# A disentangled-attention layer in a four-stage kernel: c2p rows in four buffers, c2p tables four units ahead, both skewed reads two units ahead, and fewer of stage 3's loads during attention

## The reference, cut to what matters

```
scores = einsum('bhqd,bhkd->bhqk', q, k) / scale
c2p_att = einsum('bhqd,hpd->bhqp', q, pos_k)              # 128 positions p
c2p = take_along_axis(c2p_att, clip(rel + 64, 0, 127))    # rel: bucket of q - k
p2c_att = einsum('bhkd,hpd->bhkp', k, pos_k)
p2c = swapaxes(take_along_axis(p2c_att, clip(-rel + 64, 0, 127)), -1, -2)
probs = softmax(scores + (c2p + p2c) / scale)
ctx = einsum('bhqk,bhkd->bhqd', probs, v)
```

## Time and profile before

| | us |
|---|---|
| median of 3 runs | 2724.37 |
| lowest, highest | 2719.42, 2726.56 |
| profiled execution, its own time | 2727.48 |
| its span, first to last instruction | 2725.4 |
| mean granted TensorE clock | 0.847 |

### The profile page before, as it was taken

How to read it: one execution, slowest core, us unless ns; L and a number is a source line. 1 busy time by engine, 2 the same in 40 slices (tenths; PEclk the granted TensorE clock), 3 DMA queues, 4 the chain that set the end, 5 groups by cost and what they waited for, 6 DMA issues and landing times. The chain is left out here.

```text
span 2725.4 us, 47318 instructions
## 1 busy us (share of the span) xinstructions
PE 1965.8 (72%) x13556; PEld 1445.9 (53%) x13557; DVE 1632.0 (60%) x4103; ACT 1046.4 (38%) x2098; POOL 898.0 (33%) x1079
## 2 busy tenths in 40 slices
PE   6867777777777777777769999755335159999742
PEld 3435666666666666665646666433225028877421
DVE  8946665666666566665765553577747754444344
ACT  3445554555555555555423223332001163333000
POOL 4122222222222222222232220267630015554656
PEclk9979898998988888888979999777565559999876
DMA  4679998998999899999742110000001414447333
GB/s 149 195 238 287 278 290 262 290 280 271 284 266 281 255 281 269 276 280 282 233 122 62 48 30 1 0 0 0 0 19 47 178 32 155 154 148 139 109 97 110
DMA packets 290039, 456.40 MB, mean 167 GB/s; under 512 B 38608, under 2 KB 225024, under 8 KB 289824
## 3 DMA queue, kind: packets, MB, share of 16 engines
q1 hardware_dynamic: 269344, 398.77, 48.6%
q0 software_dynamic: 16320, 42.39, 6.3%
q10 hardware_dynamic: 4160, 12.58, 1.2%
HBM read 236.67 MB, written 216.92 MB: 166 GB/s over the span
## 5 line engine op out<-in xcount | busy, mean ns | idle before, releaser
L935 DVE CUSTOM_DVE_ANT_0 probs<-bank,c2p 128x512 f32<-128x512 f32 x512 | 351.8, 687 | 425.7 <-PE bank L832 217.9
L893 ACT ACTIVATE probs<-probs,neg_max 128x512 f32<-128x512 f32 x512 | 371.5, 726 | 69.9 <-DVE neg_max L935 69.5
L908 ACT COPY a_stage<-bank 128x320 f32<-128x320 f32 (+1 forms) x512 | 211.9, 414 | 427.1 <-PE bank L801 416.3
L944 DVE COPY probsT<-bank 128x512 f32<-128x512 f32 x512 | 351.2, 686 | 11.0 <-PE bank L842 10.6
L842 PE MATMUL bank<-ident,probs 128*128 128x128 f32 x2048 | 334.7, 289 | 1.0 <-ACT probs L893 0.9
L813 PE MATMUL bank<-tab,k 96*128 96x320 bf16 (+1 forms) x512 | 165.0, 322 | 197.1 <-DVE b_stage L887 149.6
L842 PEld LDWEIGHTS bank<-ident,probs 128*128 128x128 f32 x2048 | 277.3, 152 | 13.1 <-issue 1.8
L771 POOL COPY end_c2p<-a_stage 128x4 f32<-128x4 f32 (+1 forms) x128 | 24.8, 194 | 752.0 <-ACT a_stage L908 596.9
L2122 POOL DMA_INDIRECT p_x_tile<-y_d,p_token x160 | 153.0, 956 | 329.4 <-POOLq L1813 207.4
L832 PE MATMUL bank<-ident,p2c 128*128 128x128 f32 x1280 | 249.1, 296 | 0.0
L827 PE MATMUL bank<-k,q 96*128 96x384 bf16 (+1 forms) x512 | 167.3, 327 | 91.7 <-DMA p2c<-p2c_d 66.2
(11 more groups left out here) (254 smaller groups left out, 3770.0 us busy)
## 6 DMA issues: line engine op xcount, KB each, us to landing
p2c_d<-b_stage SPq DMA_DIRECT2D x64, 640.0 KB, 4.9
c2p_d<-a_stage SPq DMA_DIRECT2D x64, 640.0 KB, 4.5
p2c_d<-b_stage SPq DMA_DIRECT2D x64, 576.0 KB, 5.2
c2p_d<-a_stage SPq DMA_DIRECT2D x64, 576.0 KB, 3.5
p2c<-p2c_d SPq DMA_DIRECT2D x256, 144.0 KB, 4.5
c2p<-c2p_d SPq DMA_DIRECT2D x256, 144.0 KB, 4.3
o_sorted_d<-p_o_pair SPq DMA_DIRECT2D x80, 256.0 KB
k<-k_stack_d SPq DMA_DIRECT2D x192, 64.0 KB
```

The lines of the kernel that those rows point to most:

```text
L893: act.activation(probs[:, w % 2, j, :], probs[:, w % 2, j, :], ACT.Exp, bias=neg_max[:, w % 2, j:j + 1], scale=-1.0).then_inc(exp_done, 1)
L908: act.copy(staged(a_stage, wa % 2, wa % TPB)[:, j, :], bank[A_BANK][:, 0:width(wa % TPB)]).then_inc(a_copied, 1)
L935: dve.tensor_tensor_reduce(probs[:, w % 2, j, :], bank[S_BANKS[(HB * w + j) % 3]][:], c2p[:, w % 2, j, :], -SCALE, LOWEST, ALU.add, ALU.mi ...
L944: dve.tensor_copy(probsT[:, wp % 2, j], bank[T_BANKS[j % 2]][:].rearrange("p (k q) -> p k q", k=TPB)).then_inc(probsT_copied, 1)
```

## The change

The c2p rows get four buffers in place of two, one to a query tile, and a semaphore each. The A tables are made and written four units ahead in place of three (A_LEAD). GpSimd fills the c2p rows of unit n+2 in place of n+1, and for that waits for the passes of unit n-2 and no longer for those of unit n-1. SyncE reads the c2p rows of unit n+2 behind the p2c rows of the same unit, and before an A write it waits until the reads of the table's last use have landed. The number of DMAs, fills, copies and matmuls in the attention's units is the same.

The four rows and w1 are no longer loaded in the attention's last body, but by SyncE at the start of stage 3, as are the row sums of sequence 1: the row bo ahead of the first inputs, the other three rows behind them, then the sums and w1. Their buffers lie among stage 3's own. GpSimd's first addition and VectorE's first step of stage 3 wait for the four rows, the reciprocal for the sums, and the first use of w1 for w1. Here is the diff, with unchanged lines cut:

```diff
@@ -522,10 +522,8 @@
...
-        rsum_in = sb(early3, "p3_rsum", [P, 2, CC, S], side="right")
+        first_sums = sb(early3, "p3_first_sums", [P, CC, S], side="right")
...
-        w1 = sb(early3, "p3_w1", [P, CC, FFN], side="right")
-        rows3 = sb(early3, "p3_rows", [P, 4, C], side="right")
@@ -540,7 +538,7 @@
...
-        A_LEAD, B_LEAD = 3, 4
+        A_LEAD, B_LEAD = 4, 4
@@ -596,7 +594,7 @@
...
-            c2p = sb(st, "c2p", [P, 2, HB, S])
+            c2p = sb(st, "c2p", [P, TPB, HB, S])
@@ -612,7 +610,7 @@
...
-            c2p_loaded = [sem("c2p_loaded0"), sem("c2p_loaded1")]
+            c2p_loaded = [sem(f"c2p_loaded{k}") for k in range(TPB)]
@@ -621,9 +619,7 @@
...
-            WEIGHTS3 = [(rows3[:, k, :], row(n)) for k, n in enumerate(("bo", "ln_scale", "ln_bias", "b2"))]
-            WEIGHTS3 += [(w[:], a[n].rearrange("(c p) n -> p c n", p=P)) for w, n in ((wo, "wo"), (w1, "w1T"))]
-            WEIGHTS3 += [(b1[:], a["b1_col"]), (scale[:], row("scale"))]
+            WEIGHTS3 = [(wo[:], a["wo"].rearrange("(c p) n -> p c n", p=P)), (b1[:], a["b1_col"]), (scale[:], row("scale"))]
@@ -675,19 +671,17 @@
...
-                        (i2, w2), (i1, w1) = ahead(i, w, 2), ahead(i, w, 1)
+                        i2, w2 = ahead(i, w, 2)
...
-                            kt = w2 % TPB
+                            t = w2 % TPB
...
-                            read_skewed(p2c_d, kt, kt, p2c[:, kt], 0, p2c_loaded[kt])
-                        if is_unit(i1, w1):
-                            t = w1 % TPB
-                            sp.wait_ge(a_written[w1 % 2], 16 * (BODY // 2 * i1 + w1 // 2 + 1))
+                            read_skewed(p2c_d, t, t, p2c[:, t], 0, p2c_loaded[t])
+                            sp.wait_ge(a_written[w2 % 2], 16 * (BODY // 2 * i2 + w2 // 2 + 1))
...
-                            sp.wait_ge(c2p_filled, BODY * i1 + w1 + 1)
-                            read_skewed(c2p_d, w1 % 4, t, c2p[:, w1 % 2], (t - 1) * P, c2p_loaded[w1 % 2])
+                            sp.wait_ge(c2p_filled, BODY * i2 + w2 + 1)
+                            read_skewed(c2p_d, t, t, c2p[:, t], (t - 1) * P, c2p_loaded[t])
@@ -700,6 +694,7 @@
...
+                            wait_count(sp, c2p_loaded[wa % TPB], 64 * (4 * ia + wa // TPB))
@@ -720,13 +715,13 @@
...
-                                    for dest, rows in ((ctx_in, slice(0, D)), (rsum_in, slice(D, 2 * D))):
-                                        sp.dma_start(dest[:, u, c], ctx_d[heads, u:u + 1, rows, :]
+                                    for dest, rows in ((ctx_in[:, u, c], slice(0, D)), (first_sums[:, c], slice(D, 2 * D)))[:2 - u]:
+                                        sp.dma_start(dest, ctx_d[heads, u:u + 1, rows, :]
...
-                    sp.wait_ge(first_ctx_loaded[1], 16 * 2 * CC)
+                    sp.wait_ge(first_ctx_loaded[1], 16 * CC)
@@ -752,14 +747,12 @@
...
-                        if is_unit(i1, w1):
-                            t, left = w1 % TPB, (w1 % TPB - 1) * P
-                            lo, hi = near_tiles(t)
-                            wait_count(pool, scores_added, HB * n)
-                            pool.wait_ge(a_ends_copied, BODY * i1 + w1 + 1)
+                            left = (t - 1) * P
+                            wait_count(pool, scores_added, HB * (n - 1))
+                            pool.wait_ge(a_ends_copied, BODY * i2 + w2 + 1)
...
-                                last = fill(c2p[:, w1 % 2], end_c2p[:, w1 % 4], side,
+                                last = fill(c2p[:, t], end_c2p[:, t], side,
@@ -786,7 +779,7 @@
...
-                    pool.tensor_tensor(ctx_in[:, 0], ctx_in[:, 0], rsum_in[:, 0], ALU.mult).then_inc(first_scaled, 1)
+                    pool.tensor_tensor(ctx_in[:, 0], ctx_in[:, 0], first_sums[:], ALU.mult).then_inc(first_scaled, 1)
@@ -928,12 +921,12 @@
...
-                                    dve.wait_ge(c2p_loaded[w % 2], 64 * (8 * i + w // 2 + 1))
+                                    dve.wait_ge(c2p_loaded[w % TPB], 64 * (4 * i + w // TPB + 1))
...
-                                    probs[:, w % 2, j, :], bank[S_BANKS[(HB * w + j) % 3]][:], c2p[:, w % 2, j, :],
+                                    probs[:, w % 2, j, :], bank[S_BANKS[(HB * w + j) % 3]][:], c2p[:, w % TPB, j, :],
@@ -948,7 +941,7 @@
...
-                    dve.reciprocal(rsum_in[:, 0], rsum_in[:, 0]).then_inc(first_inverted, 1)
+                    dve.reciprocal(first_sums[:], first_sums[:]).then_inc(first_inverted, 1)
@@ -977,12 +970,15 @@
...
-            w2 = sb(st, "p3_w2", [P, HID, C])
+            rsum_in = sb(st, "p3_rsum", [P, 2, CC, S])
+            w1, w2 = sb(st, "p3_w1", [P, CC, FFN]), sb(st, "p3_w2", [P, HID, C])
+            rows3 = sb(st, "p3_rows", [P, 4, C])
...
+            rows_loaded, next_loaded, w1_loaded = sem("p3_rows_loaded"), sem("p3_next_loaded"), sem("p3_w1_loaded")
@@ -1025,8 +1021,16 @@
...
+                    sp.dma_start(rows3[:, 0, :], row("bo")).then_inc(rows_loaded, 16)
...
+                    for k, name in ((1, "ln_scale"), (2, "ln_bias"), (3, "b2")):
+                        sp.dma_start(rows3[:, k, :], row(name)).then_inc(rows_loaded, 16)
+                    for c in range(CC):
+                        heads = slice(c * H // CC, (c + 1) * H // CC)
+                        sp.dma_start(rsum_in[:, 1, c], ctx_d[heads, 1:2, D:2 * D, :].rearrange("h b d s -> h (b d) s")
+                                     ).then_inc(next_loaded, 16)
...
+                    sp.dma_start(w1[:], a["w1T"].rearrange("(c p) n -> p c n", p=P)).then_inc(w1_loaded, 16)
@@ -1062,6 +1066,8 @@
...
+                        if isinstance(b, int) and b == 0:
+                            pool.wait_ge(rows_loaded, 16 * 4)
@@ -1213,6 +1219,8 @@
...
+                        if isinstance(b, int) and b == 0:
+                            dve.wait_ge(w1_loaded, 16)
@@ -1228,11 +1236,13 @@
...
+                    dve.wait_ge(rows_loaded, 16 * 4)
...
+                    dve.wait_ge(next_loaded, 16 * CC)
```

## The result

| | before | after |
|---|---|---|
| median, us | 2725.47 (4 runs) | 2770.99 (4 runs) |
| lowest, highest | 2719.42, 2732.45 | 2765.45, 2772.8 |
| span of the profiled execution | 2725.4 | 2768.8 |
| mean granted TensorE clock | 0.847 | 0.830 |

The ratio is 1.0163, with a 95% interval of 1.0134 to 1.0191: the change costs 45 us where I forecast a gain of 30, and 2771 lies outside my range. The forecast was wrong.

A forecast was written before the change was run, and what follows sets the result against it. The prediction took the attention loop to be paced by late c2p rows, with DMA engines 0.94 busy. Against 2727.5 us, -40 + 11 - 5 + 3 + 1 = -30 gave 2697.5, stated as 2694 us for the median, range 2656 to 2724.

The forecast's parts named there:

- c2p reads two units ahead: Attention loop: c2p waits all but vanish, gain 40 us (0 to 66), unit from 9.18 to 8.87 us.
- c2p tables four units ahead: Head group starts: c2p table matmuls wait for q rows ahead of the transposes, 11 us lost (0 to 29).
- 51 us to fill: Attention loop: of 66 us with DMA engines idle, 15 at the loop's back edges can't be filled, 51 can.
- The 7.96 us unit: Attention unit from 525.02 to 532.98, read as meeting no late transfer; the unit's arithmetic would allow 8.0 us.
- one of my three ways to be wrong: Attention loop: the forecast is wrong if p2c waits take up all that c2p gives back.
- 0.90 us a group: Head group start: TensorE work once done inside the q wait now follows it; 29 us at most over 32 groups.
- the 1.8 us at the start: Attention start: issuing of the first unit's c2p reads ahead of the second unit's p2c reads, before TensorE's start.
- the q rows decide: Rival, head group starts: c2p tables wait for q rows every group, no gain elsewhere, +28 us, 2752 us; chance 0.11.
- Its loads out of the attention: Attention's last body: row loads and w1 leave GpSimd's queue, 5 us saved (0 to 6).
- The rows at its start: Stage 3's start: first addition waits for all four rows, 512 KB more, 3 us lost (2 to 6).
- The start of the attention: First unit's c2p reads go ahead of the second unit's p2c reads, 1 us lost (-2 to 2).

The follow-up runs named there:

- E3: The kernel before with only the moved stage 3 loads, attention buffers and leads as before: 2721.38 us, ratio 0.9981 to before.
- E1: The changed kernel with the c2p tables back at three units ahead, c2p reads still two ahead: 2752.07 us, ratio 1.0088 to before.
- E2: The changed kernel with c2p rows filled and read one unit ahead again, tables still four ahead: 2747.14 us, ratio 1.0065 to before.
- E4: The changed kernel with each quarter of the q and k rows issued two units earlier: 2713.06 us, ratio 0.9948 to before.
- E9: E4 with the c2p tables three units ahead in place of four: 2720.49 us, ratio 0.9982 to before.
- E10: E4 with the quarters' loads cut to an eighth of each row from the third group on, same number of DMAs: 2706.47 us, ratio 0.9934 to before.
- E17: E14 with the quarters' loads cut to an eighth of each row from the third group on: 2610.64 us, ratio 0.9580 to before.
- E15: E5 with the quarters of the q and k rows issued by ScalarE in place of SyncE: 2728.70 us, ratio 1.0028 to before.
- E5: E3 with each quarter of the q and k rows issued two units earlier: 2721.81 us, ratio 0.9994 to before.
- E14: E4 with the quarters of the q and k rows issued by ScalarE in place of SyncE: 2690.30 us, ratio 0.9873 to before.
- E8: The changed kernel with the quarter of the q and k rows issued ahead of the c2p reads of the same step: 2724.46 us, ratio 0.9992 to before.
- E6: The changed kernel with 20 thrown-away matmuls ahead of the p2c wait at each group's first unit: 2756.02 us, ratio 1.0103 to before.

## Why the prediction was wrong

**Where it failed.** The step that failed is the part "c2p reads two units ahead", put at a gain of 40 us in bounds of 0 to 66. Taken from the medians and set on E3, these reads cost 31 us alone (E1), and 24 where the tables' lead is already longer (after less E2). The part "c2p tables four units ahead", put at 11 us lost in bounds of 0 to 29, cost 26 alone (E2) and 19 on top of the reads (after less E1): inside its bounds, near the upper one. So of the 75 us between forecast and result 64 to 71 lie in the reads, 8 to 15 in the tables, and stage 3 and the start were 3 better than I said.

The same loss can be cut another way. With the q rows out of the way both parts together are worth -8 us (E4 less E3), where I had -29, and the q rows cost 58 (after less E4). These two and E3's -4 add up to the measured 45 by construction, since each is the difference of two runs. The cost of the q rows is not a matter of the tables' lead alone: the reads by themselves bring it about as well (E1 against E9, 32 us), and I had no term for that.

**What bounds the kernel: wrong.** I read the share of 0.94 as nearly full engines with 51 us to fill. In E4 the engines were not the bound: SyncE's queue takes 8.65 to 8.72 us for a step where a unit lasts 9.05, and the same bytes taken away give 4 to 7 us there and 80 once a quarter of the issues has left the queue (E10, E17). For the kernel before, neither is shown to be the bound. Its queue waits 84.2 us in 1,100, twice as long as E4's; and relieving it brings nothing (E15 against E5), where SyncE then waits 235.4 us for the copies of the c2p table. Either limit hides the other: deeper reads are worth 0 to 8 us even with early quarters while SyncE issues everything (E9, E4), the relieved queue alone nothing (E15), both together some 30 (E14 against E3). I took bytes away in no version with reads one unit ahead.

The section of the Trainium skill that I weighed ("Perfetto Trace Analysis", "What "DMA-bound" means") names both, the engines or the queue that issues to them. The traces of E17 and E4 show one case of each, and I had tested it against the engines' share alone. By its rule the reads were worth 0, which is nearer to what they gave with early quarters, 0 to 8, than my 40.

The 7.96 us unit of the earlier trace rows was misread as well. I called it one that meets no late transfer, but the row at 532.98, which ends it, waited 1.12 us for c2p rows. Without that wait the middle units ran at 6.9 to 7.6 us, and they could not be the mean.

**c2p reads two units ahead: the c2p waits as said, the worth wrong.** The c2p waits vanished, and the p2c waits took them over, as one of my three ways to be wrong says: 164.5 us for 53.4. The units that no longer waited only came sooner to the next group's first unit, whose rows had not arrived. What the time went into there was not the p2c wait itself: it is as long in E4 and E9 (186.8 and 181.2 us), which are fast, and what those runs change is when the q rows are issued.

**c2p tables four units ahead: the mechanism right, its end missed.** The table now waits for the q rows, ahead of the transposes. I priced what TensorE loses, 0.90 us a group. What I missed is the next link: the copies come late, SyncE stands at the table's write (78 us for 43), and behind that write stand the p2c reads of the next step. I had named the queue's order, and that c2p reads stand ahead of the quarter, but priced only the 1.8 us at the start. E8 gives 46 us for that place alone. Of the rivals, "the q rows decide" names the direction and comes nearest, 17 us short, but by luck in part: its mechanism is that of the tables, 19 to 26 us of the loss, and the 24 to 31 of the reads stand in no rival.

**Not the clock.** The lower clock level fills 86 us more than before; some 15 us of the loss seem to hang on it (E6).

**Stage 3.** Its loads out of the attention: 5 us forecast, 8 measured in E3's loop, which is near what single profiles scatter. The rows at its start: 3 us forecast in bounds of 2 to 6, 5.2 measured. The start of the attention: 1 us forecast, 1.3 measured, counted from stage 1's last reciprocal.

**What stays open.** How much of E14's 22 us is SyncE's time of issuing and how much the different moment at which ScalarE issues, or that the loads no longer stand in one queue with the reads, wasn't separated, though GpSimd's version gives the same. Nor was the stall at the loop's jump back looked into. E4 and E5 differ by 9 us with intervals that touch, so the worth of the whole change without its q rows' cost, -8 us, is uncertain by about as much. How the q rows cost E1 its 31 us isn't visible in its waits.

## What to carry to other kernels

Before a wait is removed by a longer lead, find out whether the queue that issues the transfers has any time left: add up one step of its issues and gaps and hold it against the unit. If it has little, the order inside a step is worth more than its leads (46 us either way here for one swap), and what was pulled forward must not stand in front of a load that is needed next. But relieve such a queue together with the lead: each alone brought 8 us at most here, both some 30. A DMA share of 0.94, or even of 1.00, doesn't tell the engines from the queue; taking bytes away without taking DMAs away does, and it has to be done again after each change, since the limit moves.

## What the runs showed of the hardware that was not expected

- Seven hundredths of the DMA share taken away (0.95 to 0.88, E10) changed the time by 4 to 7 us of 2,713, and with a quarter fewer issues on SyncE the same bytes were worth 80 us (E17).
- The DMA share rose from 0.95 to 1.00 with the same loads on another queue, the rate and the pace staying as they were (281 and 282 GB/s, E5 and E15).
- The time is the same with the loads issued by GpSimd and by ScalarE (2691.57 and 2690.30), although ScalarE copies the tables.
- TensorE's granted clock fell to the lower level, 1.2 GHz, during its 6.19 us stall ahead of 599.49, and stayed there for 6 us and more behind it. Stretch view of after:

```profile
597.00:606.00 9.00, 4.84 (x24) 3.66 (x28) 2.77 (x7) 2.11 (x5) 0.00 (x0) 0.50 1.06 291
```
